# The last unit's mixes set between its half-sample convolutions, two of its four pairs by halves of the length

## The reference

```
# cond_128: (128, 128); conv weight: (64, 16, 9), 4 groups; experts: (8, 64, 64)
y = x + conv1d(x, weight, padding=4, groups=4) + (cond_128 @ c_weight.T)[:, :, None] + fside[None, :, None]

h   = gelu(cond_128 @ W0 + b0)
h   = gelu(h @ W1 + b1)
att = softmax(h @ W2 + b2)                      # (128, 8)
agg_w = einsum('bk,koi->boi', att, expert_w)    # one 64 x 64 matrix for each sample
agg_b = att @ bias_k
out = y + einsum('boi,bih->boh', agg_w, y) + agg_b[:, :, None]
```

## Time and profile before

| | us |
|---|---|
| median of three runs | 253.8 |
| the profiled execution's own time | 254.94 |
| its span, first to last instruction | 253.1 |
| TensorE busy | 238.5 (94%) |
| VectorE busy | 224.2 (89%) |
| ScalarE busy | 88.1 (35%) |
| GpSimd busy | 27.1 (11%) |
| moved by DMA | 68.72 MB, mean 272 GB/s |

### The profile page before, as it was taken

The page is one execution under the profiler, slowest core; times in us unless marked ns, Lnnn a source line. Parts: engine busy times, 40 slices in busy tenths (PEclk is TensorE's granted clock), DMA queues, the critical chain, the costliest instruction groups (busy, mean ns, idle before and its releaser), DMA issues.

```text
span 253.1 us, 5772 instructions
## 1 busy us (share of the span) xinstructions
PE 238.5 (94%) x2164; PEld 95.1 (38%) x2164; DVE 224.2 (89%) x148; ACT 88.1 (35%) x142; POOL 27.1 (11%) x52
## 2 busy tenths in 40 slices
PE   7379999999999999999999999999999999999970
PEld 5253233333333333333333343444443444444720
DVE  0531899999999999999999999999999999999690
ACT  2305253331423333333405142333333253222370
POOL 1021421010101010010101010101001010101000
PEclk9679999999999999999999999999999999999998
DMA  6999593999999999898979899999999896444456
GB/s 162 253 280 277 136 206 63 331 231 409 332 368 250 394 224 385 245 361 289 330 272 276 340 257 370 243 390 216 362 276 342 273 301 254 166 166 168 166 233 267
DMA packets 29483, 68.72 MB, mean 272 GB/s; under 512 B 3281, under 2 KB 5585, under 8 KB 29473
## 3 DMA queue, kind: packets, MB, share of 16 engines
q1 hardware_dynamic: 19536, 51.41, 61.5%
q10 hardware_dynamic: 9936, 17.17, 25.6%
HBM read 35.02 MB, written 33.55 MB: 271 GB/s over the span
## 4 chain that ended last, share of the span: by engine, by line
PE 89%; DMA 3%; DVE 3%; POOL 1%; ACT 1%; ACTq 0%; issue 0%; POOLq 0%
PE yps L494 63%; PE zps L517 20%; DMA zout<-in_mix_w 3%; DVE ynat L459 2%; PE zps L476 2%; PE yps L564 1%; PE yps L533 1%; DVE ycol L454 1%; PE zps L544 1%; PE zps L582 0%; ACT L325 0%; ACTq L321 0%; DVE xin L465 0%; POOL wraw L256 0%; POOL zout L252 0%
## 5 line engine op out<-in xcount | busy, mean ns | idle before, releaser
L494 PE MATMUL yps<-xph,wraw 64*64 64x512 f32 x1488 | 167.1, 590 | 0.3 <-DVE xph L387 0.3
L299 ACT ACTIVATE zout<-zps,gamu 128x512 f32<-128x512 f32 x120 | 72.7, 689 | 132.7 <-PE zps L517 89.8
L494 PEld LDWEIGHTS yps<-xph,wraw 64*64 64x64 f32 x1488 | 59.7, 132 | 100.4 <-issue 100.0
L395 DVE STREAM_TRANSPOSE ycol<-yps 128x1024 f32<-128x1024 f32 x62 | 74.5, 1220 | 9.1 <-PE yps L494 8.4
L387 DVE STREAM_TRANSPOSE xph<-xin 128x2112 f32<-128x2112 f32 x32 | 74.8, 2339 | 2.2 <-DMA xin<-in_x 2.2
L405 DVE STREAM_TRANSPOSE ynat<-ycol 128x2048 f32<-128x2048 f32 x30 | 67.6, 2290 | 1.1
L517 PE MATMUL zps<-ynat,mixv 64*64 64x512 f32 x480 | 57.3, 589 | 0.0
L235 POOL COPY mixv<-mixt 128x512 f32 (+1 forms) x16 | 17.5, 1094 | 179.0 <-ACT zout L299 174.5
L517 PEld LDWEIGHTS zps<-ynat,mixv 64*64 64x64 f32 x480 | 20.1, 132 | 31.0 <-issue 30.5
L307 ACT ACTIVATE mixt<-zps 128x1024 f32<-128x1024 f32 x8 | 7.8, 1021 | 16.9 <-PE zps L476 16.9
L564 PE MATMUL yps<-zout 128*128 128x256 f32 x20 | 8.3, 593 | 2.0 <-POOL zout L241 1.3
(11 more groups left out here) (51 smaller groups left out, 30.3 us busy)
## 6 DMA issues: line engine op xcount, KB each, us to landing
out<-zout SPq DMA_DIRECT2D x60, 512.0 KB, 5.0
xin<-in_x SPq DMA_DIRECT2D x60, 258.0 KB, 7.1
xin<-in_x ACTq DMA_DIRECT2D x60, 258.0 KB, 7.4
out<-xin SPq DMA_DIRECT2D x4, 512.0 KB, 4.9
xin<-in_x ACTq DMA_DIRECT2D x4, 132.0 KB, 4.7
xin<-in_x SPq DMA_DIRECT2D x4, 130.0 KB, 4.7
xin<-in_x SPq DMA_DIRECT2D x4, 128.0 KB, 6.1
xin<-in_x ACTq DMA_DIRECT2D x4, 126.0 KB, 5.9
```

The lines of the kernel that those rows point to most:

```text
L299: nc.scalar.activation(zout[:, o].rearrange("p (i c j q) -> p c i j q", i=2, c=2, q=PH)[:, c], zps[:, at:at + BANK].rearrange("p (q i j) - ...
L395: nc.vector.transpose(ycol[:, :, :, :, :, g].rearrange("p i s j q c -> p (i s j) q c"), yps[:, 2 * BANK * (g % 2):2 * BANK * (g % 2) + 2 * ...
L494: last = nc.tensor.matmul(yps[C * c:C * c + C, at:at + BANK].rearrange("p (s f) -> p s f", s=S // 2), wsum[rows, b, g], xph[slot][c][rows, ...
```

## The change

It rewrites the stretch after the loops.

- **TensorE.** The mixes of unit 14 no longer stand around the four half-sample convolutions but between them. The mix of pair 0 of unit 15 stands ahead of the last of them, `conv_last(1, 3)`. Then comes pair 2, whole. Pairs 1 and 3 are mixed by halves `i` of the length (`mix_half`), four matmuls of 256 columns each: both first halves, then both second halves.
- **PSUM.** Pair 0 goes to the first two banks of `zps`, pair 2 to the other two (`z_first`). The first halves of pairs 1 and 3 go to `yps`, the second halves to `zps` again, after waits on the moves of pairs 0 and 2 (`z_half`).
- **VectorE.** It moves half of pair 0 between the two pairs of short transposes of `sh = 1`, and at the end one half of pair 1. It no longer moves anything of pairs 2 and 3.
- **ScalarE.** It moves half of pair 0, all of pair 2, the first halves of pairs 1 and 3 and the second half of pair 3.
- **SyncE's queue.** Six stores in place of four: pairs 0 and 2 whole (512 KB), pairs 1 and 3 in halves of 256 KB, whose rows are 512 elements (2048 bytes) instead of 1024.

```diff
-        last_pairs = (0, 2, 1, 3)
-        def z_last(o):
-            return (yps, zps)[o % 2][:, 2 * BANK * (o // 2):2 * BANK * (o // 2) + 2 * BANK].rearrange(
-                "p (c f) -> p c f", c=2)
+        def z_first(o):
+            return zps[:, BANK * o:BANK * o + 2 * BANK].rearrange("p (c f) -> p c f", c=2)
+        def z_half(o, i):
+            return (yps, zps)[i][:, BANK * (o - 1):BANK * (o - 1) + 2 * BANK].rearrange(
+                "p (c h f) -> p h c f", c=2, h=2)[:, 0]
+        def out_half(o, i):
+            return out_last(o)[:, H * i:H * i + H]
...
+            sp.wait_ge(z_act, 1)
+            sp.wait_ge(z_dve, 1)
+            sp.dma_start(z_rows(NU - 1, 0), out_last(0)).then_inc(z_out[0], 16)
+            sp.wait_ge(z_act, 3)
+            sp.dma_start(z_rows(NU - 1, 2), out_last(2)).then_inc(z_out[2], 16)
+            for o, i, made, n in ((1, 0, z_act, 4), (3, 0, z_act, 5), (1, 1, z_dve, 2), (3, 1, z_act, 6)):
+                sp.wait_ge(made, n)
+                sp.dma_start(z_rows(NU - 1, o)[:, H * i:H * i + H], out_half(o, i)).then_inc(z_out[o], 16)
...
+            act.wait_ge(last_mixes, 1)
+            evacuate_first(0, 0)
+            act.wait_ge(last_mixes, 2)
+            evacuate_first(2, 0)
+            evacuate_first(2, 1)
+            act.wait_ge(last_mixes, 3)
+            evacuate_half(1, 0)
+            act.wait_ge(last_mixes, 4)
+            evacuate_half(3, 0)
+            act.wait_ge(last_mixes, 6)
+            evacuate_half(3, 1)
...
+            last_columns(0, 2)
+            last_columns(0, 3)
+
+            dve.wait_ge(mix_done, 4 * NU - 8)
+            last_natural(0)
+            last_columns(1, 2)
             dve.wait_ge(gam_cut, NU)
+            dve.wait_ge(last_mixes, 1)
+            nc.vector.tensor_scalar(
+                out_last(0).rearrange("p (i c j q) -> p c i j q", i=2, c=2, q=PH)[:, 1],
+                z_first(0)[:, 1].rearrange("p (q i j) -> p i j q", q=PH, i=2),
+                gamu[1][:, 0:1], None, ALU.add).then_inc(z_dve, 1)
+            last_columns(1, 3)
+            last_natural(1)
+            dve.wait_ge(last_mixes, 5)
...
             mix(NU - 2, 0, 0)
+            conv_last(0, 2)
             mix(NU - 2, 0, 1)
-            for sh in range(2):
-                conv_last(sh, 2)
-                conv_last(sh, 3)
+            conv_last(0, 3)
             mix(NU - 2, 0, 2)
+            conv_last(1, 2)
             mix(NU - 2, 0, 3)
...
```

More of the change, by code:

```diff
@@ L219, in _ @@
                     store(u, o)
[L220 to L223, removed]
+            sp.wait_ge(z_act, 1)
[6 more added lines that the diff above has]
+                sp.dma_start(z_rows(NU - 1, o)[:, H * i:H * i + H], out_half(o, i)).then_inc(z_out[o], 16)
             for o in range(PR):
-                sp.wait_ge(z_out[o], 16 * NU)
+                sp.wait_ge(z_out[o], 16 * NU + 16 * (o % 2))
         @block.gpsimd
@@ L444, in _, with last_columns, last_natural @@
                     step(2 * i - 1 + c, 1 - c)
[L446 to L449, removed]
-            for sh in range(2):
[L451 to L456, removed]
+            def last_columns(sh, g):
+                dve.wait_ge(last_conv, 2 * sh + g - 1)
+                for i in range(2):
+                    nc.vector.transpose(
+                        ycol[:, i, 2 * sh:2 * sh + 2, :, :, g].rearrange("p s j q c -> p (s j) q c"),
+                        y_last(g)[:, i].rearrange("p (n j t) -> p n t j", j=16, t=2)).then_inc(last_cols, 1)
+            def last_natural(sh):
                 dve.wait_ge(last_cols, 4 * sh + 4)
@@ L538, in conv_last, with mix_first @@
                 last.then_inc(last_conv, 1)
-            def mix_last(o):
+            def mix_first(o):
                 for c in range(2):
@@ L544, in mix_last, with mix_half @@
                         last = nc.tensor.matmul(
-                            z_last(o)[C * s:C * s + C, c].rearrange("p (n j) -> p n j", j=NJ), mixv[1][rows, 2 * o + s],
-                            ynat[1][rows, o // 2, :, :, 2 * (o % 2) + s].rearrange("p q i j -> p (q i) j"),
+                            z_first(o)[C * s:C * s + C, c].rearrange("p (n j) -> p n j", j=NJ), mixv[1][rows, 2 * o + s],
+                            ynat[1][rows, o // 2, :, :, s].rearrange("p q i j -> p (q i) j"),
+                            start=True, stop=True)
+                last.then_inc(last_mixes, 1)
+            def mix_half(o, i):
+                for c in range(2):
+                    rows = slice(C * c, C * c + C)
+                    for s in range(2):
+                        last = nc.tensor.matmul(
+                            z_half(o, i)[C * s:C * s + C, c].rearrange("p (n j) -> p n j", j=NJ),
+                            mixv[1][rows, 2 * o + s], ynat[1][rows, o // 2, :, i, 2 + s],
                             start=True, stop=True)
@@ L637, in _ @@
             mix(NU - 2, 0, 0)
+            conv_last(0, 2)
             mix(NU - 2, 0, 1)
-            for sh in range(2):
-                conv_last(sh, 2)
-                conv_last(sh, 3)
+            conv_last(0, 3)
             mix(NU - 2, 0, 2)
+            conv_last(1, 2)
             mix(NU - 2, 0, 3)
             pe.wait_ge(mixv_made, NU)
-            pe.wait_ge(last_cols, 8)
-            for o in last_pairs:
-                pe.wait_ge(last_nat, 2 * (o % 2) + 2)
-                if o % 2 == 1:
-                    pe.wait_ge(z_made, 8 * NU - 10 + 2 * (o // 2))
-                mix_last(o)
+            pe.wait_ge(last_nat, 2)
+            pe.wait_ge(z_made, 8 * NU - 10)
+            mix_first(0)
+            conv_last(1, 3)
+            pe.wait_ge(z_made, 8 * NU - 8)
+            mix_first(2)
+            pe.wait_ge(last_nat, 3)
+            pe.wait_ge(last_cols, 8)
+            mix_half(1, 0)
+            mix_half(3, 0)
+            pe.wait_ge(last_nat, 4)
+            pe.wait_ge(z_act, 1)
+            pe.wait_ge(z_dve, 1)
+            mix_half(1, 1)
+            pe.wait_ge(z_act, 3)
+            mix_half(3, 1)
 _p = np.arange(P)
```

25 lines of the change are left out of this document (15 added, 10 removed).

## The result

The changed kernel takes 253.06 us (median of 22 runs) against 253.83 us for the kernel before (22 runs). The ratio is **0.9964, with a 95% interval of 0.9951 to 0.9977**: 0.9 us faster by the ratio, 0.8 by the medians. The forecast was 252.5 us, in a range of 251.6 to 253.4, so the direction and the range hold, and the gain came out at 0.9 us instead of 1.3.

The account below looks back on a forecast made before the run. The end was taken as bound by a queue of stores delayed by an instruction fetch. Landings at 246.0, 247.25, 248.5, four halves of 0.70 and 0.5 us gave span 251.8 against 253.1, so 252.5 us, range 251.6 to 253.4.

Parts of the forecast that it names:

- What bounds the end: End of the kernel before: six 512 KB stores queued from 242.7 us, five landing 1.24 us apart after the first.
- The last issue: Last store's issue: 248.05 us instead of 247.01, hidden by the queue; the rival that it sets the end had chance 0.03.
- the late engine: One DMA engine of sixteen, held 1.64 us by an instruction fetch at 242.7 us, then working without a pause.
- The steps of every engine: After the loops: start and end times laid out for TensorE, VectorE, ScalarE and the stores, with last issue at 248.05 us.
- both pauses of TensorE: TensorE idle by half a microsecond before pair 0's mix and by 1.5 us before the half mixes.
- A half store: Stores of pairs 1 and 3 by halves: 0.70 us each, the middle of 0.62 and 0.78.
- the rival of packets priced by number: Half stores at the end: each takes 1.24 us like a whole one, time 254.7 us; chance 0.05.
- The fetch: Instruction fetch at 242.6 us in the changed kernel: unit 14's last store lands 1.85 us late, at 246.0.
- the first rival: Fetch before 242 us or in a queue hole: its 1.85 us hidden, span 251.15, time 251.9 us; chance 0.15.
- The base: Starting point of the forecast time: the 1.3 us span gain taken from the median of the runs, giving 252.5 us.
- pair 0's early mix: Ahead of conv_last(1,3): starts at 240.45 us; pair 0's store issued at 242.45 instead of 244.83 us.
- the hole from pair 2's late store: DMA hole near 245 to 246 us before pair 2's store, issued at 245.2; gives back 0.6 us more lag.

Follow-up runs that it names:

- Numbers 1 and 3: 1: the kernel before, unchanged, ratio 0.9995. 3: the kernel before with only pairs 1 and 3 of the last unit mixed, moved and stored by halves, ratio 1.0006.
- number 4: The kernel before with only unit 14's mixes put ahead of the half-sample convolutions, the last unit's pairs whole and behind the last convolution; ratio 1.0027.
- number 2: The kernel before with 12 tiny matmuls at TensorE's start, shifting its later instructions by 48; ratio 0.9998.
- Number 7: The changed kernel with pair 0's mix behind the last half-sample convolution instead of ahead; run twice, ratios to the kernel before 0.9944 and 0.9935.
- number 8: The changed kernel with conv_last(0, 3) ahead of unit 14's pair 1 mix and pair 2 by halves: ratios 0.9985, 0.9970; with 12 tiny matmuls at the start 0.9940.
- number 6: The changed kernel again, ratio to the kernel before 0.9959; and with 20 fewer TensorE instructions at the start, ratio 0.9968.

## Why the prediction was right, and where its sizes were off

- **What bounds the end: right, with one hole overlooked.** The end is set by a queue of stores, not by the last piece of work. The last issue came 1.0 us later than before (248.03 us, forecast 248.05) and the kernel is faster. Numbers 1 and 3 show the other side: there the last issue came 1.1 and 1.4 us later, and the time did not change. But the prediction had "Six stores of 512 KB start in a row at 242.7 us" and "no hole". That is true of the late engine only; the other fifteen stood still from 245.35 to 245.65 us until unit 15's first store. Without the late engine it is therefore this store, and the 2 MB from it on, that set the end of the kernel before, and bringing unit 14's stores forward was worth nothing by itself (number 4).
- **The steps of every engine: right**, to 0.1 us, with both pauses of TensorE and the transposes 2.0 us later.
- **A half store: right**, 0.69 us against 0.70. The rival of packets priced by number falls with it. The Trainium skill (DMA: Bandwidth & Descriptors, Anatomy of one DMA) gives a fixed price for each transfer on the GpSimd path. Added up store by store it would make six stores dearer than four; the trace does not bear that out for stores issued behind each other by SyncE, which ran on at 379 GB/s. The Trainium skill's full rate from 512 bytes on (DMA: Bandwidth & Descriptors, Specifications) would put the half stores at the 405 GB/s of the whole ones, an estimate; the trace is 6% below.
- **The fetch: the term that was mis-sized, twice.** The prediction said "the first store of the six [...] lands after 4.5 us [...] which is 1.9 us more than 2.6 gives", had it for 1.85 us, and carried it into the changed kernel. There the fetch came at 241.99 instead of 242.6 us, in a hole, took 0.88 us, and what was left of the lag went into the next hole. So the changed kernel's span was 251.0, not 251.8 us. That was the first rival's picture, which gave 251.15. It makes the gain larger.
- **The base: the step that made the gain too small again.** "The profiled execution took 254.94 us, 1.1 more than the median of the runs; I take the 1.3 us from the median." Those 1.1 us are about the 1.2 us of the lone engine, which by number 2 the ordinary executions of that kernel do not seem to have. Subtracting a difference of two ends, of which one has a delay that the median lacks, overstates the gain. Without the lone engine in either, the ends are 251.0 and 250.2 us, or 0.7 us when each is counted from the start of unit 15's convolutions, and 0.9 us was measured.
- **In part luck.** The two errors pull opposite ways. The whole difference of the two traces, 2.1 us, taken from the median would have been 251.7 us, at the edge of the range; without the lone engine on either side it is 253.0 to 253.1.
- **The parts are not additive.** The halves alone give +0.2 us (no change within the interval), the mixes of unit 14 alone +0.7, both with pair 0 ahead -0.9 us. The change without halves is 1.3 us slower than the kernel before. The prediction handled this right by laying out the queue as a whole; a sum of gains by part would have failed.
- **What the prediction missed** is that pair 0's early mix costs more than it brings. It listed its price, conv_last(1,3) and all behind it held up by 0.5 us of waiting and 0.86 us of mix, and named the hole from pair 2's late store, but did not ask what the queue would look like without it. Number 7 did.

## What to carry to other kernels

When the end of a kernel is a queue of stores, find its last hole: the time is the end of that hole plus the bytes behind it, and work moved forward pays only if it moves that point. Before taking a difference from a trace, compare the traced execution's own time with the median of the runs. If it stands apart, look for the event in the trace that makes up the distance, and leave it out of both sides. Where a fetch of instructions falls among the last stores, shifting the program by a few dozen instructions is worth a try; here it gave 0.9 us in one version and nothing in another.

## What the runs showed of the hardware

- A 16 KB instruction fetch held one of the sixteen DMA engines for 0.88 us in a hole (the changed kernel) and for 1.64 us among stores (the kernel before), and the stores behind it landed later by that engine until a hole let it catch up. In numbers 1 and 8 it took 0.88 us and an engine was 0.8 and 0.6 us behind at the end all the same.
- What the fetch follows is not settled. 48 more instructions of TensorE ahead of it brought it from 242.7 to 238.9 us, and from 241.9 to 237.3 us in number 8. But 20 fewer (number 6) left it at 241.95, and the same program had it at 242.7 us in one trace and at 245.85 us in another.
- Issuing a store took SyncE's queue 0.33 us, and 0.6 to 1.6 us for some that were issued while earlier stores were unfinished (numbers 1 and 3).
- Stores with rows of 2048 bytes ran at 379 GB/s, those with rows of 4096 at about 405; loads with rows of 2064 bytes at 337.
- TensorE's clock stayed at 1.00 through the pause of 1.3 us before the half mixes and was still 1.00 at 250 us, 2.8 us after its last matmul; so this pause cost no half-speed matmul here.
